# Layer 0's time recurrence on VectorE: two sets of tiles, one more wait, and another order of the five instructions of a step

## The reference, cut to what matters

```python
def step(carry, kv_t):
    aa, bb, pp = carry
    kk, vv = kv_t
    uu_kk = u + kk
    p = jnp.maximum(pp, uu_kk)
    e1 = jnp.exp(pp - p)
    e2 = jnp.exp(uu_kk - p)
    y = (e1 * aa + e2 * vv) / (e1 * bb + e2)
    ww_kk = w + kk
    pu = jnp.maximum(pp + w, ww_kk)
    e1u = jnp.exp(pp + w - pu)
    e2u = jnp.exp(ww_kk - pu)
    aa_n = e1u * aa + e2u * vv
    bb_n = e1u * bb + e2u
    pp_n = pu + jnp.log(bb_n)
    return ((aa_n, bb_n, pp_n), y)
_, ys = jax.lax.scan(step, (aa0, bb0, pp0), (k.transpose(1, 0, 2), v.transpose(1, 0, 2)))
```

```python
h = _silu_and_mul(xt @ w13_e.T)
return (y + c_e[:, None] * (h @ w2_e.T), None)
```

## Time and profile before

| what | value |
| --- | --- |
| time, median of 3 runs | 3514.79 us (3512.77 to 3516.25) |
| profiled execution: its own time, as the span of its trace | 3641.1 us |
| PE / DVE / ACT / POOL busy | 3109.3 / 2143.3 / 1398.3 / 1388.2 us (85% / 59% / 38% / 38% of the span) |
| reciprocal L789 on DVE, 512 times | 128.7 us busy, 251 ns each |

### The profile page before, as it was taken

The page is one execution under the profiler, slowest core; times in us unless marked ns, Lnnn a source line. Parts: engine busy times, 40 slices in busy tenths (PEclk is TensorE's granted clock), DMA queues, the critical chain, the costliest instruction groups (busy, mean ns, idle before and its releaser), DMA issues. The chain is left out here.

```text
span 3641.1 us, 46451 instructions
## 1 busy us (share of the span) xinstructions
PE 3109.3 (85%) x14629; PEld 1856.6 (51%) x14629; DVE 2143.3 (59%) x6568; ACT 1398.3 (38%) x3126; POOL 1388.2 (38%) x981
## 2 busy tenths in 40 slices
PE   7847897699589997999999998778996768899888
PEld 4425665466345554444444444645664445555554
DVE  4577898898344442466666654422221367887777
ACT  4424555444166663334444433111331133343331
POOL 1426100255244442012222211142004389999883
PEclk9879999799799998999999998778998878999999
DMA  5565443232310001000000000311222200000000
GB/s 194 183 221 183 144 126 123 97 113 82 99 55 1 1 1 42 7 1 18 18 18 18 18 13 12 125 67 56 87 82 90 83 0 1 12 6 7 6 6 12
DMA packets 138092, 221.08 MB, mean 61 GB/s; under 512 B 12800, under 2 KB 106240, under 8 KB 137088
## 3 DMA queue, kind: packets, MB, share of 16 engines
q1 hardware_dynamic: 99040, 146.92, 12.2%
q0 software_dynamic: 18432, 50.36, 4.3%
q10 hardware_dynamic: 20384, 20.84, 1.7%
HBM read 107.45 MB, written 110.62 MB: 60 GB/s over the span
## 5 line engine op out<-in xcount | busy, mean ns | idle before, releaser
L2307 DVE CUSTOM_DVE_ANT_0 a_ps_s<-a_ps_s,a_hide_row,a_fmax 128x384 f32<-128x384 f32 (+3 forms) x512 | 249.4, 555 | 171.1 <-PE a_ps_s L2014 170.9
L3588 POOL TENSOR_TENSOR c_prod<-c_att,c_v 128x2048 f32<-128x2048 f32 x64 | 287.4, 4531 | 27.5 <-DVE c_att L3648 27.5
L2219 POOL TENSOR_SCALAR_AFFINE_SELECT a_probs<-a_probs 128x512 f32<-128x512 f32 x128 | 79.7, 635 | 564.7 <-ACT a_probs L2496 564.7
L3588 POOL TENSOR_TENSOR c_prod<-c_q,c_k 128x2048 f32<-128x2048 f32 x64 | 286.8, 4514 | 17.3 <-ACT c_k L3999 13.7
L1515 POOL TENSOR_TENSOR a_probs<-a_probs,a_causal 128x512 f32<-128x512 f32 (+1 forms) x96 | 157.4, 1651 | 216.3 <-ACT a_probs L1744 216.3
L1744 ACT ACTIVATE a_probs<-a_ps_s 128x512 f32<-128x512 f32 (+1 forms) x384 | 170.7, 538 | 120.0 <-PE a_ps_s L1384 120.0
L2496 ACT ACTIVATE a_probs<-a_ps_s 128x512 f32<-128x512 f32 (+1 forms) x384 | 171.7, 538 | 91.7 <-PE a_ps_s L2036 91.2
L3422 PE MATMUL c_side<-c_w_e,c_h2T 128*128 128x512 f32 x448 | 202.6, 607 | 4.1 <-DVEq L3795 4.1
L2698 PE MATMUL b_ps_y<-b_w_ff,b_gelu 128*128 128x256 f32 x512 | 130.7, 406 | 59.4 <-issue 57.8
L703 PE MATMUL p_side<-p_w_expert,p_sortedT 128*128 x636 | 179.1, 406 | 0.2 <-ACT p_sortedT L838 0.2
L2875 POOL DMA_INDIRECT b_rows<-y_scratch,b_slot_int x64 | 61.7, 964 | 254.1 <-issue 239.8
(11 more groups left out here) (508 smaller groups left out, 7284.4 us busy)
## 6 DMA issues: line engine op xcount, KB each, us to landing
p_sorted_in<-sorted_scratch SPq DMA_DIRECT2D x39, 512.0 KB
y_scratch<-p_y_out SPq DMA_DIRECT2D x39, 512.0 KB
sorted_scratch<-all_zero ACTq DMA_DIRECT2D x1, 12160.0 KB, 58.3
sorted_scratch<-all_zero SPq DMA_DIRECT2D x1, 9088.0 KB, 30.7
b_sorted_in<-sorted_scratch SPq DMA_DIRECT2D x17, 512.0 KB, 4.6
y_scratch<-b_y_out SPq DMA_DIRECT2D x17, 512.0 KB, 3.2
sorted_scratch<-all_zero ACTq DMA_DIRECT2D x1, 8192.0 KB, 32.6
all_x_res<-x SPq DMA_DIRECT2D x8, 512.0 KB, 4.9
```

What stands on the lines that cost most here:

```text
L2307: last = nc.vector.tensor_tensor_reduce(out=there, in0=there, in1=hide_row[:, (TT - 1 - t) * P:], scale=HD ** -0.5, scalar=fmax[i % 2][:, ...
L3588: nc.gpsimd.tensor_tensor(out, left[:, heads].broadcast_to([P, HALF, HEADS, HD]), right.broadcast_to([P, HALF, HEADS, HD]), ALU.mult).then ...
```

## The change

The tiles `new` and `share` become pairs, `grown[0..1]` and `share[0..1]` (`bounded` in the trace), used in turn by even and odd steps. `settle` writes the state first and then the reciprocal and the share. `grow` waits twice: the ratio waits only for the state of the step before, and the weight waits for its reciprocal and share.

```diff
-        new = room.sb("new", 2, KD * B)
-        share = room.sb("bounded", 2, KD * B)
+        grown = [room.sb(f"grown{n}", 2, KD * B) for n in range(2)]
+        share = [room.sb(f"bounded{n}", 2, KD * B) for n in range(2)]
...
             def grow(t):
-
+                old, out = share[(t + 1) % 2], grown[t % 2]
+                if t:
+                    dve.wait_ge(step, ONE + 5 * t - 2)
+                nc.vector.scalar_tensor_tensor(out=out[:, 0, :], in0=scan[:, t, :], scalar=1.0, in1=scan[:, t + 1, :],
+                                               op0=ALU.add, op1=ALU.mult).then_inc(step, 1)
                 if t:
                     dve.wait_ge(step, ONE + 5 * t)
-                nc.vector.scalar_tensor_tensor(out=new[:, 0, :], in0=scan[:, t, :], scalar=1.0, in1=scan[:, t + 1, :],
-                                               op0=ALU.add, op1=ALU.mult).then_inc(step, 1)
-                nc.vector.scalar_tensor_tensor(out=new[:, 1, :], in0=share[:, 0, :], scalar=1.0, in1=share[:, 1, :],
+                nc.vector.scalar_tensor_tensor(out=out[:, 1, :], in0=old[:, 0, :], scalar=1.0, in1=old[:, 1, :],
                                                op0=ALU.min, op1=ALU.add).then_inc(step, 1)

             def settle(t):
+                at, out = grown[t % 2], share[t % 2]
                 dve.wait_ge(step, ONE + 5 * t + 2)
-                nc.vector.reciprocal(share[:, 0, :], new[:, 0, :]).then_inc(step, 1)
-                nc.vector.scalar_tensor_tensor(out=share[:, 1, :], in0=new[:, 0, :], scalar=1.0, in1=new[:, 1, :],
+                nc.vector.scalar_tensor_tensor(out=scan[:, t + 1, :], in0=at[:, 0, :], scalar=RATIO_MAX, in1=at[:, 1, :],
                                                op0=ALU.min, op1=ALU.mult).then_inc(step, 1)
-                nc.vector.scalar_tensor_tensor(
-                    out=scan[:, t + 1, :], in0=new[:, 0, :],
-                    scalar=RATIO_MAX, in1=new[:, 1, :], op0=ALU.min, op1=ALU.mult).then_inc(step, 1)
+                nc.vector.reciprocal(out[:, 0, :], at[:, 0, :]).then_inc(step, 1)
+                nc.vector.scalar_tensor_tensor(out=out[:, 1, :], in0=at[:, 0, :], scalar=1.0, in1=at[:, 1, :],
+                                               op0=ALU.min, op1=ALU.mult).then_inc(step, 1)
```

More of the change, by code:

```diff
@@ L773, in _ @@
         def _(dve):
-            nc.vector.memset(share[:, 0, :], 1.0).then_inc(share_set, 1)
-            nc.vector.memset(share[:, 1, :], 0.0).then_inc(share_set, 1)
+            nc.vector.memset(share[1][:, 0, :], 1.0).then_inc(share_set, 1)
+            nc.vector.memset(share[1][:, 1, :], 0.0).then_inc(share_set, 1)
             dve.wait_ge(share_set, ONE + 2)
             def grow(t):
+                old, out = share[(t + 1) % 2], grown[t % 2]
[3 more added lines that the diff above has]
+                                               op0=ALU.add, op1=ALU.mult).then_inc(step, 1)
```

## The result

The changed kernel takes 3486.89 us (median of 4 runs, 3478.25 to 3490.07) against 3515.52 for the kernel before: ratio 0.9916, 95% interval 0.9901 to 0.9930, which is 24.6 to 34.8 us faster. The forecast was 3479 (3465 to 3496): the result lies in its range, and the 36 us that it gave for the saving lie just above the measured interval.

What follows compares the result with a forecast made beforehand. The recurrence on DVE was taken to end the stage and so bound the kernel. DVE's 37.8 us saved, less 2 us for PE, gave 36 us off the timed 3514.79: 3479 us, range 3465 to 3496.

Steps and rivals of the forecast that it cites:

- The bound: Stage of the change: the recurrence on DVE ends it, so a microsecond taken from it is one of the kernel.
- The bare step: Recurrence step without a hide: 0.595 us against 0.69, 0.095 less; bounds 0.57 to 0.62.
- The ratio's met wait and the weight's: In grow: the ratio's already met wait costs nothing; the weight's added wait for the share costs about 0.03 us.
- Steps with a hide: Recurrence: 79 steps with a hide behind grow gain the full 0.095 us; 80 behind settle stay at 0.77, gaining nothing.
- The routing: The 34 steps among routing instructions, before 258 us: no gain, as those instructions cover the waits.
- The stalls: DVE in 258 to 400: some 26 us of long stalls, kept unchanged; bounds -13 to +13 us.
- the end of the stage "near 590": Sign of being right: the changed kernel's stage ends near 590 us instead of 626.7.
- PE: Feeding tiles to the hides: late hides behind PE's pauses lose 2 us of the gain; bounds 0 and 11.
- The rival that PE becomes the bound: Pauses come more often or grow, a tile takes about 2.0 us: 22 to 25 us saved, 3491; chance 0.10.
- the prediction's worst case: Low end of the main case: 0.07 x 398 = 28 us, less PE's 8, saves 20 us.
- Nothing gained: Rival: DVE issues the same five instructions, and waits on the one ahead are free; 3515 us, chance 0.07.
- Slower: Rival: a wait is checked only once the instruction ahead ends; step 0.80 us, 44 us lost, 3558; chance 0.03.

Runs made afterwards that it cites:

- second trace: The kernel before the change, unchanged, traced once more: 3516.99 us.
- the earlier trace: The kernel before the change, unchanged, as profiled ahead of the prediction (also "the first trace"): 3641.1 us, 126 us longer than the timed median.
- the further order: Changed kernel with the reciprocal moved between weight and state, waits adjusted: 3464.11 us, ratio 0.9845 to the kernel before the change.

## Why the prediction was right, point by point

**The bound.** Right. DVE ends the stage before and after, and what the recurrence saves is what the stage saves: 29.8 us from the end of the routing on, inside the kernel's 24.6 to 34.8.

**The bare step.** The mechanism was right, the size off. I counted 0.595 and it is 0.61. The two waits were taken as 0.03 to 0.04 and entered with the lower value: state and weight each end 0.21 behind what they wait for, not 0.20, and the rest is rounding. 398 steps x 0.015 = 6.0 us, so 31.8 instead of 37.8. It lay within the stated bounds (0.57 to 0.62), near the slow one. With some 1.6 us lost to late hides, 31.8 comes near the 29.8 that the recurrence saved, so this one term is nearly all that the forecast was too fast by. One sign was misread: the weight shows no idle time, where 0.03 was to be seen, because the ratio ahead of it is still running.

**The ratio's met wait and the weight's.** Right: the ratio overlaps the share, and one experiment that only moved its producer (0.66) and one that merged the waits (0.70) show that this overlap is the gain.

**Steps with a hide.** Right: 0.76 behind `settle` where 0.77 was forecast, 0.69 behind `grow`; moving all hides to either place made the recurrence 4.7 us shorter and 7.5 longer.

**The routing.** Right: no gain was forecast among its instructions, and the 30 steps that have one of them between two states took 38.40 us in all before (second trace) and 38.45 after.

**The stalls.** Wrong in kind. I kept 26 us of stalls as part of the kernel, and the second trace has none. By the prediction's own signs (stalls far from 26 us) this is a miss, and that it cost the forecast nothing is luck: the stalls were left equal on both sides, and the saving was taken off the timed median. But the end of the stage "near 590" had them in it: it is 569.6. That the execution was 126 us longer than the timed ones was in the table; it should have made me doubt each stall in it.

**PE.** Right in size: 2 us were allowed; the hides show 0.8 to 1.1 of waiting, and the steps with a hide took 2.0 to 2.1 us more in all than at their medians, against 0.5 before. The rival that PE becomes the bound, with pauses that grow, does not hold: at 1.9 us for a tile the pauses shrank, and at 1.76 again, though there late hides begin to count (7.0 us). The prediction's worst case took 8 us for PE where its own bound was 11; neither was reached.

**The rivals.** Nothing gained: excluded, as a step is shorter by 0.08 with the same instructions. The same five instructions took 0.69, 0.61 and 0.53 us by their order and waits, so here a count of operations doesn't give the time. In the prediction's citation of the Trainium skill, "VectorE: DVE Perf Modes", two things stand elsewhere than it says: the advice to count operations in the section "Rules for kernel authors", and the sentence that an instruction that isn't held starts earlier in "The DRAIN you can't avoid" itself. The "0.11 to 0.2 us for each wait" compares unlike instructions at its upper end; like with like it is 0.12 to 0.13 (0.21 against 0.08 to 0.09, 0.29 against 0.16). Slower: excluded, as no wait that was met left a gap.

## What to carry to other kernels

In a serial chain of small instructions on one engine, count each step by the ends of its instructions: behind a wait for the instruction just ahead, one costs its whole latency, and otherwise a fraction. Give each instruction a wait for its own producer and put between producer and consumer whatever doesn't depend on either, the longest latency above all; a new order alone, with the wait still for all of them, gains nothing. Work that already fills a wait loses that value once the wait is gone, so place it again where one is left.

## What the runs showed of the hardware

For 128x16 fp32 instructions on VectorE in these traces, an instruction without an open wait ends 0.08 to 0.09 us after the one ahead, and one that waits for it starts 0.03 to 0.04 after its end and ends 0.21 after. A wait that is already met leaves no gap: the ratio starts 0.08 before the share has ended. For the reciprocal the ends lie 0.16 and 0.29 behind the earlier trace rows. The instruction behind a reciprocal ends only 0.03 after it, whichever it is (the share in the change, the state in the further order): it lasts 0.11 there, where the same instruction elsewhere lasts 0.16 to 0.18. The long stalls of the first trace (up to 1.8 us ahead of a waiting instruction) did not come back in any of the later traces; their cause stays open, and no run here was made for it.
